# Four feed-forward tiles turned through memory, key work moved into the query steps, one store moved

## The reference

```
x = x + tanh(g_xattn[0]) * attention0(layernorm(x), ctx)   # 32 heads of 128, mask, position bias
x = x + tanh(g_ffn[0])   * ffn0(layernorm(x))              # one 512x512 product, 4-bit weights
x = x + tanh(g_xattn[1]) * attention1(layernorm(x), ctx)   # one head of 512, rms-normed q and k
x = x + tanh(g_ffn[1])   * ffn1(layernorm(x))              # 512x512 product, router, 8 adapters
```

## Time and profile before

| | before |
|---|---|
| median of 3 runs | 941.98 us (940.54 to 942.18) |
| the profiled execution | 941.42 us |
| its span, first to last instruction | 939.4 us |
| TensorE matmul (PE) busy | 931.8 us, 99% |
| TensorE weight load busy | 788.6 us, 84% |
| VectorE (DVE) busy | 600.1 us, 64% |
| GpSimd (POOL) busy | 499.2 us, 53% |
| ScalarE (ACT) busy | 403.2 us, 43% |
| chain that ended last | PE 88%, DVE 4%, DMA 2%, POOL 2% |
| mean granted TensorE clock | 1.000 |

### The profile page before, as it was taken

One profiled execution on the slowest core, in us unless ns is written; L12 is line 12 of the kernel. 1 busy time (PEld: TensorE's weight loads), 2 busy tenths in 40 slices (PEclk: granted clock), 3 DMA queues, 4 the chain that ended last, 5 costly groups with the idle time before them and its releaser, 6 DMA issues.

```text
span 939.4 us, 15355 instructions
## 1 busy us (share of the span) xinstructions
PE 931.8 (99%) x4786; PEld 788.6 (84%) x4786; DVE 600.1 (64%) x1029; ACT 403.2 (43%) x1088; POOL 499.2 (53%) x463
## 2 busy tenths in 40 slices
PE   9999999999999999999999999999999999999998
PEld 8888788888888888888888888888888888888885
DVE  4788945385538553864476546654575967768754
ACT  4765524352434334423334334433442426658730
POOL 3847574555446453646374635563456326689740
PEclk9999999999999999999999999999999999999999
DMA  7136587775777576776678666866776657337102
GB/s 287 47 122 239 194 287 269 266 264 200 260 264 269 221 268 244 269 257 257 234 259 275 258 247 223 298 232 245 263 258 251 245 200 225 135 124 228 31 1 90
DMA packets 77460, 206.79 MB, mean 220 GB/s; under 512 B 10864, under 2 KB 29808, under 8 KB 76528
## 3 DMA queue, kind: packets, MB, share of 16 engines
q1 hardware_dynamic: 76416, 205.02, 61.4%
q10 hardware_dynamic: 1008, 1.32, 0.5%
HBM read 178.00 MB, written 28.31 MB: 220 GB/s over the span
## 4 chain that ended last, share of the span: by engine, by line
PE 88%; DVE 4%; DMA 2%; POOL 2%; ACT 1%; issue 1%; SPq 1%; DVEq 0%; ACTq 0%; POOLq 0%
PE bank L2083 27%; PE bank L2099 18%; PE bank L2160 17%; PE bank L2132 6%; PE bank L2116 6%; PE bank L2265 6%; PE bank L2059 3%; PE bank L2144 1%; PE bank L2410 1%; DMA passing_keys<-kraw 1%; PE bank L2289 1%; PE bank L2003 1%; DVE work_raw L1591 1%; PE bank L2367 1%; POOL wvo L714 0%
## 5 line engine op out<-in xcount | busy, mean ns | idle before, releaser
L2160 PE MATMUL bank<-wvo,ao 128*128 128x512 f32 x768 | 179.7, 391 | 0.0
L2099 PE MATMUL bank<-wvo,ct 128*128 128x512 f32 x768 | 177.7, 390 | 0.0
L2099 PEld LDWEIGHTS bank<-wvo,ct 128*128 128x128 f32 x768 | 143.5, 188 | 29.4
L2160 PEld LDWEIGHTS bank<-wvo,ao 128*128 128x128 f32 x768 | 143.0, 188 | 29.2
L714 POOL TENSOR_TENSOR wvo<-stage,wvo 128x512 fp32r<-128x512 f32 x64 | 85.1, 1351 | 144.3 <-ACT wvo L1017 144.3
L2083 PE MATMUL bank<-ring,wkq 128*128 128x512 f32 x648 | 158.1, 391 | 0.0
L2083 PEld LDWEIGHTS bank<-ring,wkq 128*128 128x128 f32 x648 | 120.7, 188 | 24.8
L1552 DVE SCALAR_TENSOR_TENSOR acc<-bank,gated_rows,acc 128x512 f32<-128x512 f32 x128 | 93.1, 742 | 39.2 <-PE bank L2160 38.1
L1063 ACT ACTIVATE bank<-bank,nmax 128x128 f32<-128x128 f32 x256 | 88.0, 350 | 62.6 <-DVE nmax L1514 62.6
L1543 DVE TENSOR_TENSOR ao<-bank,ao 128x512 fp32r<-128x512 f32 x64 | 43.9, 691 | 99.0 <-ACT ao L1069 99.0
L1574 DVE TENSOR_TENSOR qt<-bank,qt 128x512 f32<-128x512 f32 x98 | 66.4, 690 | 56.9 <-PE bank L2083 55.5
(11 more groups left out here) (198 smaller groups left out, 1534.3 us busy)
## 6 DMA issues: line engine op xcount, KB each, us to landing
ring<-combined SPq DMA_DIRECT2D x214, 512.0 KB, 6.6
stage<-in_w SPq DMA_DIRECT2D x63, 512.0 KB, 4.3
passing<-turned_blocks SPq DMA_DIRECT2D x24, 512.0 KB, 2.9
keyed<-passing SPq DMA_DIRECT2D x96, 128.0 KB, 3.0
combined<-work SPq DMA_DIRECT2D x14, 512.0 KB, 3.6
xraw<-in_x SPq DMA_DIRECT2D x2, 1024.0 KB, 11.3
bias<-in_bias SPq DMA_DIRECT2D x8, 256.0 KB, 5.3
cs<-in_ctx SPq DMA_DIRECT2D x1, 2048.0 KB, 7.7
```

Of the source, the lines that this page charges most:

```text
L2099: mm = pe.matmul(bank[un_of[m][u] % RING][:, :], ct[:, i, c, b * P:(b + 1) * P], wvo[:, j, c, :], start=(c == 0 and i + j == 0), stop=(c = ...
L2160: mm = pe.matmul(bank[to][:, :], ao[:, h, p, b * P:(b + 1) * P], wvo[:, j, 2 * pair + h, :], start=(h == 0 and p + j == 0), stop=(h == 1 a ...
```

## The change

Four tiles of the feed-forward stage, 3 to 6, are no longer turned on TensorE. ScalarE writes each in two halves (`normed`, now two instructions, with the columns in another order), DVE turns 32x32 blocks (`ffn_turned`), SyncE passes it through a new scratch tensor (`ffn_passed`, one DMA of 256 KB; `ffn_back`, four of 64 KB) into a part of `kt1` that the keys need only later, and `hi(u, 0)` and `lo(u, 0)` read it there. In exchange `keys_back` of pairs 1 and 2 waits for `lo` of those tiles. On ScalarE `keys_weighted(0)` moves from the last feed-forward step behind `query_squares(0)`, `keys_weighted(1)` behind `probs_out(2)`; on DVE `key_turned` of tiles 3 to 7 moves later, four of them into the query steps; on GpSimd `norm(u + 4, 0)` comes first in its step. In group 0 the store `put(1, 1, 3)` moves behind `passed(0, 2)` and `back(0, 2)`. The diff, cut:

```diff
+    passing_ffn = nc.dram_tensor("passing_ffn", (4, 4, 32, 4, KC * 32), fp32, kind="Internal").ap()
...
+        def ffn_returned(u):
+            return kt1[:, (u - 1) // 2, :, :, :].rearrange("p i c t -> p (i c t)")[:, (u - 1) % 2 * D:((u - 1) % 2 + 1) * D]
+        FFN_TURNED = (3, 4, 5, 6)
+        ffn_normed = lambda u: u + 1 + min(max(u - 2, 0), 4)
...
+        turn_order = [("f", 3), ("f", 4), ("f", 5), ("t", 0), ("f", 6)] + [("t", u) for u in range(1, B)]
...
                 put(1, 0, 2)
-                put(1, 1, 3)
                 passed(0, 2)
                 back(0, "first", 2)
+                put(1, 1, 3)
...
+                    elif pair:
+                        sp.wait_ge(S["lo0"], 2 * pair + 3)
...
+                def ffn_passed(u):
+                    sp.wait_ge(S["T1"], ffn_turns[u])
+                    sp.dma_start(passing_ffn[u - 3, :, :, :, :].rearrange("i k j c -> (i k) j c"),
+                                 xnr[:, normed_slot(u, 0), :].rearrange("p (j c) -> p j c", j=4)).then_inc(s_fpassed, 16)
+                def ffn_back(u):
+                    if u >= 5:
+                        sp.wait_ge(s_fback[u % 2], FBASE + 64)
+                    sp.wait_ge(s_fpassed, FBASE + 16 * (u - 2))
+                    for j in range(4):
+                        sp.dma_start(ffn_returned(u)[32 * j:32 * j + 32, :].rearrange("k (i c) -> k i c", i=4),
+                                     passing_ffn[u - 3, :, :, j, :].rearrange("i k c -> k i c")).then_inc(s_fback[u % 2], 16)
...
@@ GpSimd @@
                 for u in range(B):
+                    if u < 4:
+                        norm(u + 4, 0)
                     if 0 < u < 5:
                         key_root(u + 2)
...
-                    if u < 4:
-                        norm(u + 4, 0)
...
@@ ScalarE, normed @@
-                    if n == 0 and u >= 2:
+                    if n == 0 and u >= 5:
+                        act.wait_ge(s_fpassed, FBASE + 16 * (u - 4))
+                    elif n == 0 and u >= 2:
                         act.wait_ge(S["T0"], u - 1)
...
+                    if n == 0 and u in FFN_TURNED:
+                        dst = dst.rearrange("p (e j c k) -> p e j c k", e=2, j=2, c=KC)
+                        src = src.rearrange("p (j k c e) -> p e j c k", j=2, c=KC, e=2)
+                        for e in range(2):
+                            act.activation(dst[:, e, :, :, :], src[:, e, :, :, :], ACT.Identity, bias=nmr[:, u:u + 1],
+                                           scale=rs1[:, u:u + 1]).then_inc(S["xn0"], 1)
+                        return
...
@@ ScalarE, the list @@
+                normed(3, 0)
                 for u in range(B):
+                    if u + 1 in FFN_TURNED:
+                        hi(u + 1, 0)
...
-                    if u < 5:
-                        normed(u + 3, 0)
-                    if u < 6:
+                    if u in (0, 5):
                         hi(u + 2, 0)
-                    else:
+                    elif u >= 6:
                         hi(u - 6, 1)
+                    if u < 4:
+                        normed(u + 4, 0)
...
-                    elif u == 7:
-                        keys_weighted(0)
...
                     query_squares(u)
+                    if u == 0:
+                        keys_weighted(0)
...
@@ DVE @@
+                def ffn_turned(u):
+                    dve.wait_ge(S["xn0"], ffn_normed(u))
+                    blocks = xnr[:, normed_slot(u, 0), :].rearrange("p (f k) -> p f k", k=32)
+                    dve.transpose(blocks, blocks).then_inc(S["T1"], 1)
...
@@ DVE, the list @@
                 for u in range(B):
+                    if u + 1 in FFN_TURNED:
+                        lo(u + 1, 0)
                     if u:
                         x2(u - 1)
-                    if u < 6:
+                    if u in (0, 5):
                         lo(u + 2, 0)
...
-                    if 0 < u < 6:
+                    if 0 < u < 4:
                         key_turned(u - 1)
+                    elif u == 5:
+                        key_turned(3)
+                    if u < 4:
+                        ffn_turned(u + 3)
...
```

More of the change, by code:

```diff
@@ L390, in build @@
         halves = lambda u: [slice(0, D)] if u < B - 1 else [slice(0, D // 2), slice(D // 2, D)]
+        turn_order = [("f", 3), ("f", 4), ("f", 5), ("t", 0), ("f", 6)] + [("t", u) for u in range(1, B)]
+        ffn_turns = {u: turn_order.index(("f", u)) + 1 for u in FFN_TURNED}
+        tile_turns = {u: turn_order.index(("t", u)) + 1 for u in range(B)}
         key_tile = lambda u: kraw[:, u // 2 % 3, :, :, u % 2, :].rearrange("p j c k -> p (j c) k")
@@ L668, in _ @@
                 tile_back(0)
+                ffn_passed(6)
+                ffn_back(6)
                 tile_passed(1)
                 tile_back(1)
-                keys_passed(1)
                 tile_passed(2)
@@ L1275, in hi @@
                 def hi(u, n):
+                    if n == 0 and u in FFN_TURNED:
+                        act.wait_ge(s_fback[u % 2], FBASE + 64 * ((u - 3) // 2) + 64)
+                        act.wait_ge(S["y0"], u - 1)
+                        act.activation(tt[:, slot(u, 0), 0, :, :].rearrange("p c (i t) -> p i c t", i=4),
+                                       ffn_returned(u).rearrange("p (i c t) -> p i c t", i=4, c=KC),
+                                       ACT.Copy).then_inc(S["hi0"], 1)
+                        return
                     if n == 1:
@@ L1404, in _ @@
                         probs_out(u - 3)
+                    if u == 5:
+                        keys_weighted(1)
                     if u >= 5:
```

48 lines of the change are left out of this document (29 added, 19 removed).

## The result

The changed kernel takes **947.45 us** (median of 5 runs, 946.46 to 948.88); the kernel before took 941.82 us beside it (5 runs, 940.54 to 942.18). The ratio is 1.0064, with a 95% interval of 1.0053 to 1.0075: 5.6 us slower. The forecast was 944.0 with a range up to 946.0, so the sign was right and the size was not.

What follows compares the result with a forecast made beforehand. The prediction took the matmul engine (PE), busy 99% of the span, as the bound. Terms -1.2 (store), +1.9 (tile 6), +1.1 (weighted keys) and +0.2 summed to +2.0, giving a median of 944.0 us, range 940.5 to 946.0.

Steps and rivals of the forecast that it cites:

- the store: Group 0: with the store behind the probabilities' write, PE's wait of 1.5 us shrinks; -1.2 us, bounds 0 and 1.5.
- tile 6: Feed-forward stage: tile 6 returns late through SyncE's queue, at 843.5, delaying x2(5) and ffn(7); +1.9 us, +1.0 to +2.6.
- DVE and GpSimd: Feed-forward tiles: lo reading from kt1 contends with GpSimd, the pace of tiles 3 to 5; +0.2 us, bounds 0 and 1.8.
- the weighted keys: Turn of query 1: ScalarE's copy of query 0 comes later behind four weightings; +1.1 us, bounds 0 and 2.55.
- the term at `ffn(7)`: Last feed-forward step: ffn(7) waits for x2(5), late behind tile 6; +1.9 us.
- 2.6 us could go here. That is the ceiling.: Feed-forward stage: most PE could gain from four turned tiles, 2.0 us, and its waits of 0.6; not a summed term.
- GpSimd's pace: Feed-forward stage: GpSimd's list, without pause from 818.20, takes 15.8 us, ends norm(7, 0) at 834.0; ffn(5) starts at 838.7.
- Later steps are paced by PE again and I cost them at nothing.: Behind the turn of query 1, including the second weighting moved behind probs_out(2): no cost, 0 us.
- the queue as the bound: Rival: late landings and GpSimd's contention together, store's gain down to 0.5; +4.8, 946.8 us; chance 0.12 with another worse rival.
- The marks named as right: Signs: waits for acc at ffn(5) to ffn(7) of 4 to 6 us, for qtr about 1; all 2 us late after.
- A mark named as wrong: Signs against: feed-forward waits under 2 us in all, tile 6 back before 841, or a PE wait in another place.

Runs made afterwards that it cites:

- e2: The changed kernel with the store put(1,1,3) back in its old place; 948.57 us, +7.1 over the kernel before.
- e1: The kernel before with only the store put(1,1,3) moved behind passed(0,2) and back(0,2); 940.38 us, -1.1 against the kernel before.
- e8: The kernel before with one TensorE transpose instead of four for each of tiles 3 to 6; 941.24 us, -0.7 against the kernel before.
- e4: The changed kernel with tile 6's write issued in front of tile 0's four reads; 946.04 us, +4.6 over the kernel before.
- f1: The changed kernel with only tiles 3, 4 and 5 through memory, tile 6 turned by TensorE again; 944.15 us, +2.5 over the kernel before.
- f3: The kernel before with only the two keys_weighted moved to their new places on ScalarE; 943.95 us, +2.3 over the kernel before.
- g3: The kernel before with only the first keys_weighted moved, behind the squares of query 0; 942.68 us, +1.4 over the kernel before.
- e5: The changed kernel with tile 4's write issued in front of keys_back(1); 946.30 us, +4.3 over the kernel before.
- g1: The kernel before with the store moved, only tiles 3 and 4 through memory and the changed kernel's GpSimd norm order; 942.10 us, +0.9.
- c1: The changed kernel with tile 6's and tile 4's writes issued sooner and GpSimd's last two low parts behind its step 4; 945.21 us, +3.2.
- g2: The kernel before with only a pause added: five unused DVE statistics reads in front of x2(3); 945.15 us, +3.9 over the kernel before.
- f4: f1 with tile 4's write in front of keys_back(1) and GpSimd's last two low parts behind its step 4; 943.84 us, +2.2.
- h2: g1 with GpSimd's last two low parts and SyncE's router weights load later, and features from step 3; 943.45 us, +1.8 over the kernel before.

## Why the prediction was wrong

Right in sign and in most places, 3.5 us too low in size. The spans of the two traces lie 6.3 apart, and this can be laid beside the forecast's terms, place by place:

| place | forecast, us | traces, us |
|---|---|---|
| up to the first turn behind the loop (the store) | -1.2 | -0.7 |
| from there to `ffn(7)` (tile 6, and DVE and GpSimd) | +2.1 | +3.4 |
| from `ffn(7)` to the turn of query 1 (the weighted keys) | +1.1 | +2.7 |
| behind it | 0 | +0.9 |

(Each trace is one execution. That of e2, whose lists behind the loop are the changed kernel's, has 3.8 and 3.6 in the second and third row.) So the steps that failed are the term at `ffn(7)`, 1.3 too low, the term of the weighted keys, 1.6 too low, and the later steps that were put at nothing. Step by step:

- **The store, -1.2.** Right: -1.1 in e1, the wait 1.5 to 0.2. (The trace of the changed kernel is 1.1 ahead right behind the wait and only 0.7 at 810 us; that of e1 is 1.2 ahead there. What took the 0.4 is open.)
- **"2.6 us could go here. That is the ceiling."** Too high. e8 gave 0.7 for 1.5 of work, and nothing hung on it in the sum.
- **GpSimd's pace.** Right in clock time, by luck: `norm(7, 0)` was forecast to end at 834.0 and ended at 834.3; `ffn(5)` was forecast for 838.7 and began at 839.0. But the list took 16.8 us (817.45 to 834.27) and not 15.8: the two splits with the step to the next instruction 3.1 instead of 2.55, the five norms 6.6 instead of 6.3 (at the forecast's own 1.3 each they would have been 6.5), the feature 1.4 instead of 1.3. It ended on time only because the store let it start 0.75 sooner than in the earlier trace rows, and the forecast booked the store's gain as a term while it counted its clock times from the old start. With the store undone (e2) the norm ends at 835.19 and `ffn(7)` begins at 851.73, 4.2 behind the earlier trace rows (0.4 of it there from the first microseconds on) and not 1.9. This is the first step that failed; it hides 0.7 of the loss at `ffn(7)`. Nor is GpSimd without a pause from 818.20 on in the kernel before, though no sum rests on that:

```profile
822.52 0.23 POOL L889 TENSOR_SCALAR small<-mv 128x1 f32<-128x1 f32 x1 [2.12 <-DVE mv L1661]
```

- **DVE and GpSimd, +0.2 (bounds 0 and 1.8).** Too low, and looked for at the wrong engine. `lo(4)` took 1.63 beside a feature, not 0.7, and made most of the wait of 1.2 in front of `ffn(4)` that the forecast did not have; the splits took 2.99 beside `lo(3)`, not 2.55. The rule of the Trainium skill that the forecast weighed (GPSIMD Engine Reference, Key points: the two share SBUF interfaces) holds here: for tiles 3, 4 and 5 one of the two instructions that ran beside each other is longer, and the price falls on either engine (2.99 for the splits beside `lo(3)`, 1.63 for `lo(4)`, 1.73 for the feature beside `lo(5)`); beside `lo(6)`, 0.69, GpSimd was idle. How much of the 1.3 at `ffn(7)` this is, no run took apart.
- **Tile 6, +1.9 (range +1.0 to +2.6).** The queue was read right: written at 837.08 (forecast 837.3). The tile was turned only at 835.96, not 834.8, so a free queue would have won 1.1 at most (e4: 0.9). The reads came 2.56 us behind the write and their issue took 2.87, so the copy began at 844.23 and not 843.5, the late end: this is the other 0.7 of the loss at `ffn(7)`. f1 prices the tile: 3.1 us, since its five DMAs also delay what is queued behind them, which the forecast did not follow past `x2(5)`.
- **The weighted keys, +1.1.** DVE's list from `x2(5)` to the read of query 0 took 7.9 (forecast 7.7). The copy was forecast done 13.4 behind `x2(5)` and was done at 14.9 (849.40 to 864.28). The missing 1.5 is tile 4's write, held behind `keys_back(1)`. For the weightings alone the 1.1 is right: from `ffn(7)` to the turn of query 1 lie 11.5 us in the kernel before, 12.6 in f3 and g3, 13.0 in e5 and 14.2 in the changed kernel. The forecast charged a moved step on ScalarE and did not look at what the moved step in SyncE's list holds up there.
- **"Later steps are paced by PE again and I cost them at nothing."** Wrong by 0.9 in the trace: 0.4 at the scores behind the turn of query 1, as in f3 and g3, and 0.4 at those of query 4, where the second weighting is not done (f3 has that, g3 not; in the medians f3 less g3 is 0.9).

In the medians the store is -1.1, both weightings are +2.3 and tile 6 is +3.1; of the +5.6 that leaves 1.3 for the other three tiles. No run measured those three by themselves, and the parts need not add: g1 less e1 puts 2.0 on tiles 3 and 4 alone. The forecast had -1.2, +1.1 and +2.1 for all tiles. The rival "the queue as the bound" (946.8) came nearest in its number, but for a reason that did not hold: it let the store's gain go, and the store kept it. The marks named as right were there (5.3 us of waits for `acc`, a wait for `qtr`), but the second was 2.5 and not 1, and the whole was 5.6 and not 2 late. A mark named as wrong was there too, a wait of TensorE in another place: 1.2 in front of `ffn(4)` and 0.6 in front of the scores of query 4.

Left open: how much of the changed kernel's median the slow clock carries (its five executions do not separate), and why tile 6's reads were issued only 2.56 and, in c1, 3.59 us behind its write, where the earlier trace rows have 2.1; more transfers share the engines at that time, but no run took them away alone. Open too is why g1's executions lie 2.4 apart, where the slow clock adds 1.6 to the twelve matmuls of its profile.

## What to carry to other kernels

When work leaves an engine that is 99% busy, what comes out is bounded by the next chain in line; try it first with the work simply left out, as e8 did, before any of the new path is built. A step that is moved must be followed on every in-order queue to the last one that waits, and clock times must not be carried from the old trace into a kernel whose start has shifted. Measure the parts of a mixed change alone: here the small one was the only gain.

## What was not expected of the hardware

- A pause of TensorE can cost more than its length: some 1.3 us on top of 2.6 in g2, 2.4 between executions of g1, where the matmuls behind it run at 1.2 GHz (4.6 us for twelve instead of 3.0). It strikes most executions of some kernels and none of others (f4, with a longest wait of 1.5 behind the loop, stayed at 0.999 to 1.000 in all eleven). The profiles of the changed kernel, e5 and h2 have waits of 2.1 to 2.9 and no slow stretch.
- A VectorE subtraction with both inputs in SBUF took 1.63 and 1.81 us beside a GpSimd multiplication, against 0.69 alone: the loss on VectorE can be twice that on GpSimd (1.73 instead of 1.29).
- A set of four DMA issues on SyncE mostly takes 1.7 to 2.1 us, but now and then more, up to 2.96 in the kernel before, 2.98 in the changed one (849.31; 2.87 at 839.64 above) and 3.52 in e5, with no wait on a semaphore between the four. One such set lay on the path of tile 6.
